# Cross attention's chain re-timed in a fused decoder: keys and values earlier, shorter gaps between its steps, exponentials kept in two banks

## The reference, cut to what matters

```python
x = x + L2_ffn(layernorm(x))      # two "bit linear" layers around a GELU
x = x + L3_attn(layernorm(x))     # 16 heads of 64; softmax(k q^T / 8), then wo
# L3 cross attention, for each token l: 16 heads of 8 numbers, and the softmax is
# over the 16 heads g of the SAME token
q, k, v = layernorm(x) @ Wq.T + bq, ctx @ Wk.T + bk, ctx @ Wv.T + bv
energy = einsum('nhld,ngld->nlhg', q, k)
attn   = softmax(energy / sqrt(128), axis=3)
out    = einsum('nlhg,ngld->nhld', attn, v)
x = x + ((layernorm(out) * ln_g + ln_b) @ Wo.T + bo)
```

## Time and profile before

| | us |
|---|---|
| three runs | 1133.72, 1133.14, 1127.75 (median 1133.14) |
| the profiled execution, its own time | 1128.98 |
| its span, from the first to the last instruction | 1127.2 |
| TensorE busy in the span | 838.1 (74%) |
| VectorE busy | 611.0 (54%) |
| ScalarE busy | 350.3 (31%) |
| GpSimd busy | 317.2 (28%) |

### The profile page before, as it was taken

The page is one execution under the profiler, slowest core; times in us unless marked ns, Lnnn a source line. Parts: engine busy times, 40 slices in busy tenths (PEclk is TensorE's granted clock), DMA queues, the critical chain, the costliest instruction groups (busy, mean ns, idle before and its releaser), DMA issues. The chain is left out here.

```text
span 1127.2 us, 16031 instructions
## 1 busy us (share of the span) xinstructions
PE 838.1 (74%) x5969; PEld 605.2 (54%) x5977; DVE 611.0 (54%) x1430; ACT 350.3 (31%) x687; POOL 317.2 (28%) x319
## 2 busy tenths in 40 slices
PE   5974787983657185589887686689999998348895
PEld 2542453573434074367664444367777777234894
DVE  2654862323299952467566776575435455753222
ACT  1110574330112111116445463134434233111331
POOL 1344100203138724122221111000034262435132
PEclk9985898895678677669998788689999999659897
DMA  9302200360000004406356000000000000004685
GB/s 373 130 1 83 71 5 1 108 182 19 20 0 1 0 1 84 94 20 130 79 136 183 17 3 1 1 1 2 2 2 1 2 1 1 1 1 151 203 300 162
DMA packets 44679, 72.44 MB, mean 64 GB/s; under 512 B 4818, under 2 KB 36738, under 8 KB 43034
## 3 DMA queue, kind: packets, MB, share of 16 engines
q1 hardware_dynamic: 38921, 65.72, 19.7%
q0 software_dynamic: 1728, 3.59, 0.9%
q10 hardware_dynamic: 3952, 2.10, 0.7%
HBM read 58.65 MB, written 15.89 MB: 66 GB/s over the span
## 5 line engine op out<-in xcount | busy, mean ns | idle before, releaser
L847 DVE TENSOR_REDUCE space<-PS 128x2 f32<-128x512 f32 x128 | 83.5, 686 | 40.7 <-PE PS L651 40.4
L2546 DVE TENSOR_REDUCE space<-PS 128x2 f32<-128x512 f32 x64 | 43.5, 691 | 95.8 <-PE PS L2243 95.7
L831 ACT ACTIVATE annex<-PS 128x384 f32<-128x384 f32 (+1 forms) x128 | 67.5, 544 | 63.6 <-PE PS L662 33.9
L2282 PEld LDWEIGHTS PS<-space 128*128 128x128 f32 x512 | 62.2, 193 | 18.2 <-issue 16.7
L2262 PE MATMUL PS<-space 64*128 64x256 f32 x256 | 71.6, 411 | 0.0
L2282 PE MATMUL PS<-space 128*128 128x65 f32 x512 | 69.8, 282 | 0.2 <-ACT space L2364 0.2
L2243 PE MATMUL PS<-space 64*128 64x256 f32 x256 | 68.7, 444 | 0.1
L1950 POOL TENSOR_TENSOR space<-space 128x1536 f32<-128x1536 f32 x16 | 54.7, 3443 | 37.9 <-DVE space L1881 31.7
L1170 PE MATMUL PS<-space 128*128 128x128 f32 x444 | 55.5, 278 | 2.7 <-ACT space L1239 2.4
L2364 ACT ACTIVATE space<-PS 128x512 f32<-128x512 f32 x64 | 37.3, 597 | 63.0 <-PE PS L2263 62.8
L1170 PEld LDWEIGHTS PS<-space 128*128 128x128 f32 x444 | 51.7, 192 | 4.9 <-issue 3.6
(11 more groups left out here) (493 smaller groups left out, 2232.9 us busy)
## 6 DMA issues: line engine op xcount, KB each, us to landing
space<-in_e_l_ffn SPq DMA_DIRECT2D x22, 768.0 KB
space<-in_e_l_ffn SPq DMA_DIRECT2D x23, 192.0 KB, 2.6
l_ffn_sorted<-in_slots SPq DMA_DIRECT2D x2, 1584.0 KB, 25.6
space<-l_attn_scratch_k SPq DMA_DIRECT2D x8, 384.0 KB
space<-l_ffn_sorted SPq DMA_DIRECT2D x10, 264.0 KB, 4.8
weights<-in_w_l_xattn SPq DMA_DIRECT2D x1, 2504.0 KB, 15.2
weights<-in_w_l_attn SPq DMA_DIRECT2D x1, 2124.0 KB, 11.9
space<-l_xattn_scratch_q SPq DMA_DIRECT2D x4, 512.0 KB, 3.5
```

Source lines behind the costliest of these rows:

```text
L831: nc.scalar.activation(P[:, u % 8, 0:keys], PS[:, 3 + u % 2, 0:keys], ACT.Exp).then_inc(exp_done, 1)
L847: nc.vector.tensor_reduce(m[:, :, at_h], max_bank(u).rearrange("p (c k) -> p c k", c=2), AX_X, ALU.max).then_inc(max_done, 1)
L2282: last = nc.tensor.matmul(out, p[:, 256 * kc + 128 * qc:256 * kc + 128 * qc + 128], VB[:, b % 2, kc, h, :], start=kc == 0, stop=kc == 1)
L2546: nc.vector.tensor_reduce(MX[:, half % 2, :, h], PS[:, max_bank[a], :].rearrange("p (c k) -> p c k", c=2), AX_X, ALU.max).then_inc(max_don ...
```

## The change

It does three things. (1) `exp_bank` keeps to banks 3 and 4 to the end, the wait for all maxima ahead of unit 47 goes, and ScalarE waits for them ahead of its copies to banks 0 and 1 (and 3 and 4). (2) Cross attention of each batch begins in the step of job `o..5`, not in the next one, with its keys and values two steps and one step ahead of that. (3) The gaps between its pieces are cut: from `xq` to `xo` 12 steps in place of 15 for batches 0 and 1, and 9 in place of 15 for batches 2 and 3, and batch 2's `xw` stands five steps behind its `xo`. How the maxima are placed is the same in both kernels (eight heads at a time).

```diff
-    exp_bank = [3 + i % 2 if i < ALONE else (0, 1, 3, 4)[(i - ALONE) % 4] for i in range(UNITS)]
+    exp_bank = [3 + i % 2 for i in range(UNITS)]
...
-    first_x = [job_at["o", b, 5] + 1 for b in range(B)]
+    first_x = [job_at["o", b, 5] for b in range(B)]
...
-        place(f, "xk", b, 0)
-        place(f + 1, "xv", b, 0)
+        place(f - 2, "xk", b, 0)
+        place(f - 1, "xv", b, 0)
         piece(f + 1, "normedx", b)
         f = place(f + 2, "xT", b, 0)
         f = place(f + 1, "xq", b, 0)
-        for i, what in ((1, "products"), (3, "sum0"), (5, "sum1"), (5, "shift"), (6, "expx"), (7, "dens"), (7, "values"),
-                        (9, "weigh0"), (12, "weigh1"), (12, "scale"), (13, "out"), (14, "normedo")):
-            if b in SHARED and what[:-1] in ("sum", "weigh"):
-                continue
-            piece(f + i, what, b)
-            if b in SHARED and what in ("products", "values"):
-                piece(f + i, "sum1" if what == "products" else "weigh1", b)
-                piece(f + i, "sum0" if what == "products" else "weigh0", b)
-        f = place(f + 15, "xo", b, 0)
-        place(f + 1, "xw", b, 0)
+        if b in SHARED:
+            for i, what in ((0, "products"), (0, "sum1"), (0, "sum0"), (2, "shift"), (3, "expx"), (4, "dens"), (4, "values"),
+                            (4, "weigh1"), (4, "weigh0"), (6, "scale"), (7, "out"), (8, "normedo")):
+                piece(f + i, what, b)
+            f = place(f + 9, "xo", b, 0)
+            place(f + (5 if b < B - 1 else 1), "xw", b, 0)
+        else:
+            for i, what in ((1, "products"), (3, "sum0"), (4, "sum1"), (4, "shift"), (5, "expx"), (6, "dens"), (6, "values"),
+                            (8, "weigh0"), (9, "weigh1"), (9, "scale"), (10, "out"), (11, "normedo")):
+                piece(f + i, what, b)
+            f = place(f + 12, "xo", b, 0)
+            place(f + 1, "xw", b, 0)
...
-                if i == ALONE:
-                    pe.wait_ge(max_done, UNITS)
...
                 if b in SHARED and kind != "xk":
+                    act.wait_ge(max_done, UNITS)
                     nc.scalar.copy(PS[:, SHARED[b] + (kind != "xq"), 0:128], out[:, 128:256]).then_inc(beside, 1)
```

## The result

The kernel after the change takes **1167.02 us** (median of 4 runs, 1162.80 to 1168.96); the kernel before 1133.43 in the same comparison (4 runs, 1127.75 to 1139.47). The ratio is **1.0291, 95% interval 1.0230 to 1.0351**: slower, as forecast, but by 33 us and not by 6, and outside the range. That the direction came out right is largely luck: the mechanism forecast gives some 5 to 7 of the 33 us. The profiled execution is 1168.96 long, its span 1167.1.

A forecast was written before the change was run, and what follows sets the result against it. TensorE alone was taken to set the pace under the heads, a chain mostly on VectorE the stage's end. The terms summed to +6.3 us, put on a mean of 1130.9: 1137.2 us, range 1130 to 1142.

The forecast's parts named there:

- A: TensorE under the heads: moved jobs 1.1 us, a wait for batch 0's x 1.8, banks 0.2; 3.1 us later in all.
- wait for batch 0's x: Under the heads, TensorE waits for VectorE's normalised x before batch 0's `xT`: 1.8 us, ends 0 and 3.3.
- B: Start of batch 2's products in the tail: 1.28 us gained by earlier `xT` and `xq`; start at 953.05 us.
- G: Batch 3's chain, from its products to the stage's end: 24.4 us, ending at 1006.9 against 1000.63.
- banks: Two exponential banks under the heads: TensorE waits 0.2 us at the first pair, nothing waits later.
- rival 3: The clock falls under the heads too: +7.8 us, 1138.7 us in all; chance 0.05.
- C: Last `normalise`, now behind batch 2's products and two sums (7.17 us): batch 3's `t` and `o` jobs start 10 us later.
- D: Tail: batch 2's `expx` stands behind three `t` copies, half clock adding 1.5 us; starts at 967.8, VectorE waiting 5 us.
- rival 1: The clock holds at 2.4 GHz through the tail's `t`, `o` and `xq` jobs: +3.6 us, 1134.5; chance 0.18.
- rival 2: In the tail `expx` is not held and starts at 962.2, so the change is not slower: 1129.8 us; chance 0.10.
- E: Tail, from `expx` to the end of batch 2's weighing: 8.5 us, ending at 976.3 against 975.59.
- F: Batch 3's `cross` to queries, no longer hidden by batch 2's weighing: 6.25 us; batch 3's products start 6.8 us later.

The follow-up runs named there:

- the second profile of the change: The changed kernel itself run and profiled once more, nothing altered: 1161.37 us, ratio 1.0341 to the kernel before.
- `xT` a step later: The changed kernel with two added waits on GpSimd and batch 0's `xT` placed one step later: 1129.08 us, ratio 1.0048 to the kernel before.
- the two waits: The changed kernel, GpSimd's first `products` and batches 0 and 1's `values` made to wait for VectorE's writes: 1147.41 us (ratio 1.0191), again 1141.91 (1.0149).
- the old gaps back: The changed kernel with the old, longer gaps for batches 0 and 1 only, early start kept: 1146.28 us, ratio 1.0230 to the kernel before.
- the early memsets alone: The kernel before with GpSimd's three memsets at the stage's start moved ahead of the first two deviations: 1124.55 us, ratio 0.9983.

## Why the prediction was wrong

**The step that failed is A**, TensorE under the heads, put at 3.1 us, with 4.6 as its high end (1.1 + 3.3 + 0.2). It counted the work that was moved and one wait, and put what the moved products and values of batches 0 and 1 do to VectorE at nothing. In the stage of the second profile of the change the sum is:

| | predicted | measured, by the stage |
|---|---|---|
| VectorE held by GpSimd, three times | not there | 401.7 - 379.2 = **22.5** |
| wait for batch 0's x, with the clock behind it (`xT` a step later) | 1.8 (3.3) | 379.2 - 371.5 = **7.7** |
| everything else (B to G, moved jobs, banks) | 4.5 | 371.5 - 366.6 = **4.9** |
| sum | 6.3 | 35.1 |

Each row is the difference of single profiles. By the medians the first is 14.0 us in the one comparison (1161.37 - 1147.41) and 20.6 across the two (38.3 - 17.7). It is not VectorE's 22 us of standstill either, though the numbers are alike: what costs is TensorE's time. In the second profile of the change TensorE stands 14.3 us for the held instructions (6.20, 2.17 and 5.95), and works for 22.3 us at the low clock behind these waits (836.3 to 845.5, 876.3 to 879.7 and 934.8 to 944.5 us), where half is lost: 11 us, an estimate from these rows, 25 with the waits. In the second row, 2.19 us are the wait and 3.3 the low clock behind it (half of 6.6 us of work, an estimate too); the rest is not explained by it.

- **The collisions.** I took durations of VectorE's instructions from the earlier trace rows and looked at what each waits for, never at what runs on GpSimd at that time. The trace of before shows a held pair at 634 us, and 0.60 for the same line elsewhere: the evidence was there. The statement of the steps was at hand too: `values` came to stand in the steps of the maxima's parts. For an engine that "has half of the time free" I priced moved work at nothing. Shown by removing them (the two waits), by shortening GpSimd's instructions, and by making them (18.8 us from four tiny instructions).
- **The wait for batch 0's x.** Its mechanism is right and its length nearly so (2.19 us, 1.8 forecast). Wrong was what follows: rival 3, that the clock falls under the heads too, had 0.05. Against it I had put's wait of 0.96 us, which is no evidence for one of twice that length. The clock fell in this wait, or within 1.4 us of its end, in all nine profiles that have it. Length alone doesn't decide, though: in the run with the old gaps back, waits of 1.92 and 2.11 us (at 894.83 and 921.87) brought no fall.
- **The banks** show no cost (0.2 forecast, with some 2.7 us to either side as the interval).
- **B.** From the start of the last exponential (978.51 us after, 946.85 before) to batch 2's products it is 3.15 us after and 4.38 before: 1.23 gained, 1.28 forecast.
- **C.** The last `normalise` starts 7.05 us behind the products (7.17), and the `t` jobs follow it, behind 7.31 us of idle time.
- **D.** `expx` starts 6.1 us behind `shift` (5 or more), 15.1 us behind the products (14.75), with the first `t` and `o` jobs at half the clock: rival 1, by which they would not be, and rival 2, `expx` not held, are out.
- **E and F.** The weighing is over 23.6 us behind the products (23.25), batch 3's products start 30.4 behind (29.45): F's chain took 6.8 us (1005.28 to 1012.04), not 6.25.
- **G.** 24.4 us from there to the end, as forecast.

So every sign that the prediction named for being right came true, all of them in the tail, and the sum was still short by 27 us: no sign reached to where they were lost. The tail itself, from batch 2's products to the end, took 54.8 to 56.0 us in all profiles with the new steps for batches 2 and 3, and 48.2 to 50.9 in those with the old ones.

Rival 1 leant on the Trainium skill ("TensorE: Matmul & The Clock Gate", Part 1), by which the clock's ramp costs under 1% of a typical kernel's span and is not to be fitted. Each piece here is that small: 1.4 us in the tail (3.39 for 2.02 of work), 3.3 behind the wait for batch 0's x, 11 behind the collisions, of 1161 us, the last two by the estimates above. Together they are over 1%, and twice what the whole change was forecast to cost, so in this case they can't be left out.

## What to carry to other kernels

Before moving work on GpSimd, list what VectorE will do while each long GpSimd instruction runs: a tensor_scalar or an instruction with two SBUF inputs that is issued meanwhile lasts until GpSimd's ends, however small it is, and what waits for VectorE in its order waits too. Price it by the engine that sets the pace: where that is TensorE, add a stretch at the low clock behind its wait (TensorE's waits for held instructions, 2.17 to 6.20 us in the profiles of the change, all had one). And a step in a table orders one engine's queue only: an engine with nothing else to do runs ahead to its long instruction, and what parts it from the other engine's small one is a wait.

## What was not expected of the hardware

- A GpSimd memset, which reads nothing, holds a tensor_scalar too: 3.32 us for the pair beside a memset of 3.51.
- A stretch at the low clock is not the same length in each execution of one order: from 747 us on it lasted 30.7 us in the first profile of the change (mean 0.51), in one of the two with the two waits and in that of the early memsets alone, and 10.2 us (mean 0.85 in the second profile of the change), or two times 3.4, in the other fifteen. The long one is worth 8.4 us, about the scatter between executions of one kernel.
